# A two-layer recurrence on TensorE: input products in tiles of 64 stationary columns instead of 32

## What is computed

```python
x = x + _L0_cond_ref(cond_1024, x, ...)   # GRU-like recurrence over the 256 times
x = x + _L1_cond_ref(cond_1024, x, ...)   # second recurrence over the 256 times
x = x + _L2_cond_ref(x, cond_1024, ...)   # gated cumulative sums
x = x + _L3_cond_ref(x, cond_1024, ...)   # conditioned low-rank adapter

def step(h, xs):                          # of the first layer
    xzt, xrt, xht = xs                    # x @ W_z, x @ W_r, x @ W at this time
    z = jax.nn.sigmoid(xzt + h @ U_z + vz)
    r = jax.nn.sigmoid(xrt + h @ U_r + vr)
    hh = jnp.tanh(xht + r * h @ U + vh)
    h_new = (1.0 - z) * h + z * hh
    return (h_new, h_new)

def step(h, z_t):                         # of the second layer
    gate = jax.nn.sigmoid(h @ Wh.T + z_t @ Wz.T + b)
    h_new = jnp.tanh(h * leak + gate * z_t)
    return (h_new, h_new)
```

## Time and profile before

| what | value |
|---|---|
| median of 3 runs | 992.34 us (991.52 to 993.38) |
| the profiled execution's own time | 988.54 us |
| its span, first to last instruction | 986.7 us |
| mean granted TensorE clock | 0.979 of 2.4 GHz |
| busy: TensorE (matmul), TensorE (weight load) | 939.5 us (95%), 763.6 us (77%) |
| busy: VectorE, ScalarE, GpSimd | 803.9 us (81%), 647.4 us (66%), 203.3 us (21%) |
| share of the chain that ended last: TensorE, VectorE, ScalarE | 55%, 31%, 4% |
| recurrence (loop L865) | from about 17 us to about 611 us |

### The profile page before, as it was taken

The page is one execution under the profiler, slowest core; times in us unless marked ns, Lnnn a source line. Parts: engine busy times, 40 slices in busy tenths (PEclk is TensorE's granted clock), DMA queues, the critical chain, the costliest instruction groups (busy, mean ns, idle before and its releaser), DMA issues.

```text
span 986.7 us, 112657 instructions
## 1 busy us (share of the span) xinstructions
PE 939.5 (95%) x50966; PEld 763.6 (77%) x50966; DVE 803.9 (81%) x2468; ACT 647.4 (66%) x2862; POOL 203.3 (21%) x390
## 2 busy tenths in 40 slices
PE   5699999999999999999999999959999999999986
PEld 5699999999999999999999998325555555555554
DVE  2378778878788778777878887799999999999993
ACT  2477777777777777777777776336455556555552
POOL 0011111111111111111111111223333223323330
PEclk7699999999999999999999999979999999999999
DMA  6113312310010100100101001100010000001001
GB/s 219 41 57 111 111 47 98 110 35 27 24 37 24 37 24 27 35 27 24 37 24 37 24 27 33 28 1 25 24 42 29 24 24 24 24 24 48 24 24 43
DMA packets 38295, 42.02 MB, mean 43 GB/s; under 512 B 5120, under 2 KB 31232, under 8 KB 37120
## 3 DMA queue, kind: packets, MB, share of 16 engines
q1 hardware_dynamic: 36832, 40.55, 13.3%
q10 hardware_dynamic: 1440, 1.18, 0.4%
HBM read 32.80 MB, written 8.91 MB: 42 GB/s over the span
## 4 chain that ended last, share of the span: by engine, by line
PE 55%; DVE 31%; issue 8%; ACT 4%; DMA 1%; ACTq 1%; DVEq 1%; POOL 0%; POOLq 0%
PE bank L772 30%; PE bank L718 22%; DVE arena L645 10%; DVE wx L657 4%; DVE cx L661 4%; ACT cand_kept L369 2%; DVE cx L670 2%; DVE cx L674 2%; DVE wx L643 2%; DVE cx L666 2%; DVE none_h L582 2%; DMA bias<-in_bias 1%; PE bank L890 1%; PE bank L907 1%; PE bank L861 1%
## 5 line engine op out<-in xcount | busy, mean ns | idle before, releaser
L718 PE MATMUL bank<-x_ahead,wx 128*32 128x64 f32 x12376 | 345.6, 224 | 6.4 <-ACT bank L336 3.2
L718 PEld LDWEIGHTS bank<-x_ahead,wx 128*32 128x32 f32 x12376 | 240.1, 111 | 3.3 <-issue 3.3
L772 PE MATMUL bank<-none_h,urz 128*32 128x32 f32 x16384 | 203.2, 199 | 8.6 <-issue 5.0
L772 PEld LDWEIGHTS bank<-none_h,urz 128*32 128x32 f32 x16384 | 180.8, 110 | 27.7 <-DVE none_h L582 13.2
L267 POOL TENSOR_TENSOR x<-x_f,h_gx 128x64 f32 x256 | 87.4, 341 | 529.9 <-PE bank L772 528.8
L890 PE MATMUL bank<-x,wl 128*128 (+1 forms) x384 | 180.9, 610 | 0.9 <-DVE rank_rows L624 0.9
L772 PE MATMUL bank<-rh_f,uh 128*32 128x32 f32 x8192 | 151.6, 199 | 5.0 <-DVE rh_f L570 2.2
L890 PEld LDWEIGHTS bank<-x,wl 128*128 128x128 f32 x384 | 68.7, 190 | 88.1 <-issue 88.1
L772 PEld LDWEIGHTS bank<-rh_f,uh 128*32 128x32 f32 x8192 | 122.7, 112 | 7.1 <-DVE rh_f L570 5.3
L582 DVE TENSOR_TENSOR_SCAN none_h<-zero_z,cand_kept 128x64 f32<-128x64 f32 x512 | 121.4, 278 | 5.4 <-ACT cand_kept L369 4.0
L380 ACT ACTIVATE h_gx<-h_pre 128x64 f32<-128x64 f32 x256 | 68.8, 269 | 80.8 <-DVE h_pre L608 80.8
(11 more groups left out here) (87 smaller groups left out, 1290.0 us busy)
## 6 DMA issues: line engine op xcount, KB each, us to landing
x_in<-in_x SPq DMA_DIRECT2D x34, 256.0 KB, 2.7
x_ahead<-in_x SPq DMA_DIRECT2D x130, 64.0 KB, 1.9
arena<-in_w SPq DMA_DIRECT2D x8, 1024.0 KB, 5.7
out<-y SPq DMA_DIRECT2D x32, 256.0 KB, 2.5
rank_rows<-in_bias_rows SPq DMA_DIRECT2D x1, 1024.0 KB, 5.0
arena<-scratch SPq DMA_DIRECT2D x64, 16.0 KB
cx<-in_cx SPq DMA_DIRECT2D x1, 768.0 KB, 4.5
wx<-in_wx SPq DMA_DIRECT2D x1, 768.0 KB, 6.6
```

The lines of the kernel that those rows point to most:

```text
L718: mm = pe.matmul(out[32 * j:32 * j + 32], weights(k, j, m), moving(k), start=False, stop=False, tile_position=(0, 32 * j), skip_group_chec ...
L772: mm = pe.matmul(out[32 * j:32 * j + 32], weights(k, j, m), moving(k), start=False, stop=k == 1, tile_position=(0, 32 * j), skip_group_che ...
```

## The change

The helper `ahead` takes a width. The first input products, ahead of the loop, keep 32 stationary columns; all others have 64, so that two tiles cover the array instead of four, each with the same 64 moving columns. The four slabs of 32 columns of a weight do not lie beside each other in `wx` and `wz1`, so GpSimd copies them in the beginning into `wx_wide` (in the space of `cx`, whose last reader is done by `const_pre`) and `wz_wide` (in the space of `y`), in 8 copies of 128x256. TensorE waits for them (`widened`) ahead of the loop. The order of `turn` stays as it was.

```diff
+WIDE = 2 * BLK
...
+        wx_wide = cx[:].rearrange("p k j g e -> p (k j g e)").rearrange("p (g k m n) -> p g k m n", g=3, k=HALVES, m=HALVES)
+        wz_wide = y[:, 0].rearrange("p h t -> p (h t)").rearrange("p (k m n) -> p k m n", k=HALVES, m=HALVES)
...
+            def widen(dst, src):
+                slabs = lambda w: w.rearrange("p j (m c) -> p m j c", m=HALVES)
+                pool.tensor_copy(dst.rearrange("p m (j c) -> p m j c", j=SLABS), slabs(src)).then_inc(widened, 1)
+
+            pool.wait_ge(wx_in, 16)
+            pool.wait_ge(const_pre, 1)
+            for gate in (0, 2):
+                for k in range(HALVES):
+                    widen(wx_wide[:, gate, k], wx[:, k, :, gate])
+            pool.wait_ge(weights_in, 16 * len(WEIGHT_LOADS + SECOND_LOADS))
+            for k in range(HALVES):
+                widen(wz_wide[:, k], wz1[:, k])
+            for k in range(HALVES):
+                widen(wx_wide[:, 1, k], wx[:, k, :, 1])
...
-            def ahead(out, m, weights, moving, parts=range(HALVES)):
+            def ahead(out, weights, moving, width, parts=range(HALVES)):
 
                 for k in parts:
-                    for j in range(SLABS):
-                        mm = pe.matmul(out[32 * j:32 * j + 32], weights(k, j, m), moving(k), start=False, stop=False,
-                                       tile_position=(0, 32 * j), skip_group_check=True)
+                    for at in range(0, P, width):
+                        mm = pe.matmul(out[at:at + width], weights(k, at), moving(k), start=False, stop=False,
+                                       tile_position=(0, at), skip_group_check=True)
                 return mm
 
-            def ahead_first(par, gate, m, parts=range(HALVES)):
+            def ahead_first(par, gate, m, parts=range(HALVES), first=False):
 
                 out = (pre_rh[par][m][:, 0], pre_z[par][:, m], pre_rh[par][m][:, 1])[gate]
-                return ahead(out.rearrange("p v b -> p (v b)"), m,
-                             lambda k, j, m: wx[:, k, j, gate, m * BLK:(m + 1) * BLK],
-                             lambda k: x_ahead[:, par, :, k, :], parts)
+                narrow = lambda k, at: wx[:, k, at // BLK, gate, m * BLK:(m + 1) * BLK]
+                wide = lambda k, at: wx_wide[:, gate, k, m, at:at + WIDE]
+                return ahead(out.rearrange("p v b -> p (v b)"), narrow if first else wide,
+                             lambda k: x_ahead[:, par, :, k, :], BLK if first else WIDE, parts)
 
             def ahead_second(at, par):
 
                 for m in range(HALVES):
-                    ahead(pre_g[par][:, m].rearrange("p v b -> p (v b)"), m, col(wz1),
-                          lambda k: x1_f[:, at:at + STEPS, k, :])
+                    ahead(pre_g[par][:, m].rearrange("p v b -> p (v b)"), lambda k, at: wz_wide[:, k, m, at:at + WIDE],
+                          lambda k: x1_f[:, at:at + STEPS, k, :], WIDE)
...
             pe.wait_ge(weights_in, 16 * len(WEIGHT_LOADS + SECOND_LOADS))
+            pe.wait_ge(widened, 8)
```

More of the change, by code:

```diff
@@ L152, in build_program @@
         rank_loaded = [sem("rank_loaded0"), sem("rank_loaded1")]
-        pad_done = sem("pad_done")
+        pad_done, widened = sem("pad_done"), sem("widened")
         l2_pre, f_done, i_done, c_done = sem("l2_pre"), sem("f_done"), sem("i_done"), sem("c_done")
@@ L757, in _ @@
             for gate, m in ((0, 0), (0, 1), (2, 0), (2, 1)):
-                ahead_first(0, gate, m)
-            ahead_first(0, 1, 0)
-            ahead_first(0, 1, 1, (0,)).then_inc(ahead_loaded[0], -16)
+                ahead_first(0, gate, m, first=True)
+            ahead_first(0, 1, 0, first=True)
+            ahead_first(0, 1, 1, (0,), first=True).then_inc(ahead_loaded[0], -16)
             pe.wait_ge(hidden_in, 16 * len(HIDDEN_LOADS))
```

## The result

The changed kernel takes **1156.96 us** (median of 4 runs, 1153.76 to 1157.54), the kernel before 992.86 us (4 runs, 991.52 to 994.45). The ratio is 1.1651, 95% interval 1.1625 to 1.1678: slower by 164 us, where 1179 us were forecast, within the range of 1070 to 1220. The profiled execution has a span of 1155.5 us, 168.8 us over the 986.7 us of before.

The account below looks back on a forecast made before the run. TensorE was taken to bound steps after long blocks, the state's way through other engines those after short ones; 988.54 + 203.5 for width changes - 17 of slack gave 1175 us, as a median 1179, range 1070 to 1220.

Parts of the forecast that it names:

- The streaming brings nothing: Input products in the loop: two wide tiles take the same 59 ns per round as four narrow ones, no gain.
- The price of a change: Six tile-width changes per step: 0.146 us to 64 columns, 0.119 back to 32, 0.795 per step, 203.5 us.
- The rivals of half the price and of none: Width changes in the loop: half price, 1077 us, chance 0.10; no price and faster, 981 us, chance 0.17.
- The 51 ns of exposed load: First record behind a change to 64 columns: 51 ns longer, interpolated between 24 for 32 columns and 104 for 128.
- The slack: TensorE's idle time behind short blocks: 0.135 us used up in each of two steps per turn, 17 us off.
- a branch "which stays": At the loop's end, the rest of TensorE's idle time (0.25 - 0.135) was taken for the branch and stays.
- its 0.83 us from the candidate to the gates at the loop's end: Time by way of tanh and scan, against 0.86 for a short block with two changes, so the chain stays on TensorE.
- The start: GpSimd's copies ahead of the loop: 0.63 us each, last ends at 16.2, hidden; counted 0, bounds 0 to 1.6 us.
- The cap of the faster rival: No price per change: every step takes 2.16 us, plus 0.12 at the loop's end; at most 11 us gained; chance 0.17.
- The clock: Rival: TensorE idles 0.57 us more per step in six gaps, the clock halves, 1690 us; chance 0.03.
- The 3.8 us that were added for the median: Whole kernel: the median of runs lies 3.8 us over the profiled execution, turning 1175 into 1179 us.

Follow-up runs that it names:

- experiment 5: The change, but all products of the loop, the state's too, with 64 stationary columns from host-laid weights, no GpSimd copies: 1131.76 us, ratio 1.1399.
- experiment 6: The change with tiles of 128 stationary columns for input products: 1983.45 us; such tiles only behind the candidate, two changes per step: 1190.76 us.
- experiment 1: The change with its copies, wait and new weight place kept, but all input products in tiles of 32 again: 991.34 us, ratio 0.9996.
- experiment 2: The change with input products wide only in the candidate's middle: 1063.8 us; only behind the candidate: 1032.38 us; in both places: 1096.94 us.
- experiment 7: The kernel before, all narrow, with four input products moved from each long block to the short one: 995.04 us; with two turns per loop body: 1955.17 us.
- layout_only: The run of experiment 1: the change's copies and weight layout, but tiles of 32 throughout: 991.34 us, ratio 0.9996.

## Why the prediction was right, and which terms were off

1. **The streaming brings nothing.** Right, and slightly worse than said. A wide block of 20 records takes (403.01 - 402.43 - 0.049 - 0.007) / 9 = 0.058 us per round (0.80 us less 0.22 gives the last start, 403.01). The forecast took 59 ns from a block of 39, which holds an irregular start; inside that block seven rounds follow each other in 0.39 us, 0.056 each. So wide rounds lose about 2.5 ns, 16 x 256 x 0.0025 = 10 us. Experiments 5 and 6 show the cause: at 64 columns the load takes as long as the 64 moving columns (0.055 us per round even with 32 moving), and at 128 twice as long (0.112).
2. **The price of a change.** Right in place and size: 0.146 and 0.119 us forecast, from rows of other pairs of tiles; 0.096 + 0.049 = 0.145 and 0.096 + 0.021 = 0.117 measured, once the 0.03 and 0.055 us that the last records stream are taken off the gaps of 0.125 and 0.151. The Trainium skill, TensorEngine Tiling (Array Packing), section Key Properties, has a change of tiling mode drain TensorE; here the trace agrees also between 32 and 64 columns, with 0.096 us in which nothing starts, which no row before showed. The rivals of half the price and of none are out by experiments 1 and 2. The 51 ns of exposed load, between 24 for 32 columns and 104 for 128, came out at 49 partly by luck: experiment 6 measured 48 for 128 columns, so it does not grow with the columns as that line had it.
3. **The slack was mis-sized**, the one step that failed. "That is all the slack in a turn", 0.27 us used and 0.115 for a branch "which stays". Per turn, three changes each way in four steps are 12 x 0.262 = 3.14 us and the slower rounds 0.16; measured are 4 x 0.669 = 2.68. So 0.63 us of a turn was covered, 0.36 more than counted, 23 us in all. The gates' starts over all steady steps tell where (mean us, each step up to the next gates):

   | step of the turn | before | after | longer by | changes and rounds | covered |
   |---|---|---|---|---|---|
   | 0, long block | 2.271 | 3.039 | 0.768 | 0.83 | 0.06 |
   | 1, short block | 2.157 | 2.800 | 0.643 | 0.82 | 0.18 |
   | 2, long block | 2.276 | 3.033 | 0.757 | 0.83 | 0.07 |
   | 3, short block and the loop's end | 2.293 | 2.800 | 0.507 | 0.82 | 0.31 |

   Steps 1 and 3 were counted with 0.135 each. Step 3 has the branch's 0.13 on top of what step 1 covers; it is gone with wide blocks ahead, and why it is hidden there isn't shown. The prediction had the number for it in hand: its 0.83 us from the candidate to the gates at the loop's end, against 0.86 with the changes, contained the branch, and so only 0.03 could be lost there. It read that stretch as the state's way, from the chain's scan up to 305.38; but that is the second scan, and the first gates wait for the first alone, over at 305.18 (experiment 7). In step 0 it is a longer step once in 16, 2.45 us before (gates at 287.27 and 289.72), which is gone. It stands where ScalarE's and VectorE's own loops of 16 steps turn, and the reset gate's sigmoid starts 0.80 us behind the gates there (288.07) and 0.65 in the step from 300.81; no run tests that cause. The rest are gaps of 0.02 to 0.08 us between starts behind the gates and ahead of the candidate in the trace before, which the modelled ends of the records cover up in the views that group them; in the changed kernel the one ahead of the candidate is 0.015, and a change of width stands in place of the other.
4. **The start.** Copies hidden, right: 0.40 us each, not 0.63, and the last starts at 15.3. Not foreseen: the first 16 steps lost 4.4 us in place of 16 x 0.669 = 10.7. TensorE's waits for nothing that the profile shows ("issue" as releaser), most likely for its own code, were, in the kernel before, from 20 to 50 us:

```profile
PE bank L772 <- issue: 6.3, 4, 2.7
PE bank L718 <- issue: 3.2, 2, 2.1
```

   and in the changed kernel, from 17 to 60 us:

```profile
PE bank L793 <- issue: 1.5, 2, 1.2
PE bank L737 <- issue: 1.4, 1, 1.4
```

   That is 6.6 us less, which fits the difference of 6.3, with a sixth of the loop's matmuls gone; no run tests it. Of the 3.8 us in the rest, 0.9 come with the last step and what follows it in the recurrence. The others are within what this stretch varies by: 378.0 us in the profile before is the shortest of all the kernels here, and `layout_only`, whose instructions there are the same, has 380.5. The 0.6 us ahead of the loop is no different: 17.17 us before, 17.68 in the run of experiment 7, which copies nothing.
5. **The cap of the faster rival** (every step at 2.16 us, 11 us gained) rested on the same reading of the branch. Experiment 7 gave 0.4% slower instead. It did not bear on the forecast.
6. **The clock** stayed at 1.00 in the steady steps with six gaps in each, as taken; it did fall to 0.50 in the run with tiles of 128, but the rival's mechanism, idle gaps, isn't shown by that: the changed kernel has six gaps per step as well and kept 1.00.

The forecast's excess, against the profiled 168.8 us: 187 less 23 (slack), less 6 (first steps), less 2 (price), plus 10 (rounds), plus 3 and 1 (behind and ahead of the loop) gives 170. The 3.8 us that were added for the median did not come again: the profiled execution of the changed kernel took 1157.32 us, the median 1156.96. So 1179 us was 22 too many, and as a part of the 164 us it was close because the faults are small beside a price that was right.

No run beat the kernel before: `layout_only` ties with it, the two other narrow ones (experiment 7) and all with a wide tile lost.

## What to carry to other kernels

Count how often the stationary tile's shape changes in the inner loop before widening a part of the matmuls, and price each change from any place in the trace where the shape changes: the time in which nothing starts, plus what the first record behind it is longer. Merging tiles that already ran side by side saved instructions here, not array time (0.058 us per round for 0.056); with 32 moving columns the wider load even became the pace. Slack is read from starts over a whole period of all engines' loops (here 16 steps), branch and rare steps included, not from one gap, and a wait is measured from the instruction that the semaphore names.

## What the hardware showed that was not expected

- TensorE's granted clock stayed at half (0.50, 1.2 GHz) through the whole recurrence with input products in tiles of 128 columns in all three places of a step, although the profile calls the engine 100% busy; with such tiles in only one of the three places it was full in the steady part (mean 0.981).
- A loop body twice as long (8 steps in place of 4) took the queue of instruction fetches from 0.20 to 6.90 MB and nearly doubled the kernel's time, with the granted clock at 0.76 in the stretch shown.
- The extra time at TensorE's loop branch, 0.13 us behind narrow blocks, did not show behind wide ones: 0.15 us from the last record to the gates with the branch and without it.
- The first record behind a change is 0.049 us longer than its fellows with 64 stationary columns and 0.048 with 128 (64 moving columns each).
